# The shared expert of all batches worked in the last turn and behind the experts, with new turn orders; last results fetched by SyncE

## The chip, the cores and the metric

The kernel runs on one core of a Trainium2 chip. A core has TensorE (PE: matrix products, from SBUF into the eight banks of PSUM), VectorE (DVE), ScalarE (ACT), GpSimd (POOL) and SyncE (SP). Each works its instructions in the order in which they are written, and waits on counters (semaphores) that others raise. Data between HBM and SBUF go by DMA, issued by SP, ACT or POOL. The metric is the device time of one execution in microseconds (us).

## What is computed

Eight batches of 256 tokens with 256 channels go through four steps, each followed by a layer norm of input plus result:

```
x = layernorm(x + L0_attn(x))   # q, k, v; convolution of 3; long convolution by FFT; Wo
x = layernorm(x + L0_ffn(x))    # 16-head causal attention, modulated MLP of 1024
x = layernorm(x + L1_attn(x))   # q * cumsum(k * v), Wo
x = layernorm(x + L1_ffn(x))    # mixture of experts, below

probs = softmax(x @ gate_w.T);  topk_w, topk_idx = top_k(probs, 6)      # of 64 experts
routed_out = sum over the 6 of topk_w * (silu(x @ w1[e].T) @ w2[e].T)   # inner width 176
g, u = split(x @ shared_gate_up.T)                                      # 352 each
shared_out = silu(g) * u @ shared_down.T                                # the shared expert
return routed_out + shared_out
```

Everything is in float32 but for a few split operands.

## The kernel before

**Turns.** The first three steps and the routing are a pipeline over batches. Stage A is the first step, C and B the second (C: the queries and keys; B: units u0 to u15 of attention, MLP f0 to f7, B8), D the third step with routing, G the scatter of the rows of a routed batch to their experts' places in HBM. One turn works A of batch n, B of n-1, D of n-2 and G of n-3. A table of part names (`TURN`) sets the order, and each engine runs those of its parts that stand in it. There are turns -1 to 9. Turn 1 has its own table (no D yet), turn 8 is `LAST_BUT_ONE` (no A), turn 9 is `LAST` (only D and G). So D, and with it the shared expert, stands in turns 2 to 9.

**Attention units.** In a unit TensorE makes scores (L772), DVE their maxima (L1340), ACT the exponentials (L1070), DVE the reciprocal of their sums, POOL multiplies (`prob<-prob,rec`, L564). Three units later TensorE transposes (L659) and ACT copies (probT), and one unit further TensorE makes the values (L790, L796). The G scatters (L589) stand between POOL's multiplies, as do the inverse roots of the norms (L572: yA, yB, yD, yR).

**The shared expert.** x3, the output of step three, is transposed to x3T. S0, S1 and S2 are gate and up products in tiles of 128, 128 and 96 columns (L893, bank 7), each with a tanh on ACT (L1124) and two products on DVE (L1458, L1461) that give sact. SDa and SDb are the down product (L912), SD adds it to x3 into X (L1490). In the last turn S0 stands between DTa and DTb, the two parts that work out the table of experts for the chunks; the others stand behind DTb.

**Behind the turns.** SP waits for the table to load expert weights, and for the last scatter (D6, 12 scatters of batch 7 from x_row) to load rows. 40 quads of 4 chunks of 128 rows follow: transposes (L659), inner products (L962, L968), outer products (L979, L983), the scatter of the results to y_rows by POOL (L627). At last 16 tiles are finished: ACT issues the load of a tile's six results per token (`collect`, L1149), makes diagonal weights (`weigh`, L1157) and issues the store (`put`, L1166), all in one queue; TensorE sums five of the six (L995), DVE adds the sixth, X and the sum (L1589, L1592) and norms. There are four load buffers and two output buffers (`outb`).

Of the kernel before, what the change touches and what calls it, by code (L numbers as in the profile page):

```python
# [28 lines left out]
P = 128  # L29
NB, L, D = 8, 256, 256  # L30
KT = D // P
# [101 lines left out]
def build(nc, d):  # L133
# [6 lines left out]
    with ExitStack() as ctx:  # L140
# [96 lines left out]
        sgt, sgs, sact = sb("sgt", [P, L]), sb("sgs", [P, L]), sb("sact", [P, len(SH_TILES), L])  # L237
        hit = sact[:].rearrange("p n l -> p (n l)").rearrange("p (t k e) -> p t k e", t=TT, k=TOPK)

        zeros = sgt  # L240
# [17 lines left out]
        def ring(n, *shape):  # L258
# [25 lines left out]
            "d_rank d_pos d_dest d_copied d_scat d_sg d_sgt d_sact d_sd d_base "  # L284
            "ch_a ch_b ch_d ch_r ch_f r_tot r_tab r_row r_table r_fill "
            "m_w0 m_x0 m_w1 m_x1 m_w2 m_x2 m_w3 m_x3 m_ids ch_m r_spot r_all m_xT m_xT_out m_h m_hs m_y m_y_out m_st0 m_st1 m_st2 m_st3 "
            "f_ld0 f_ld1 f_ld2 f_ld3 f_st0 f_st1   f_diag f_sum f_r f_out n_varF n_invF").split()}
# [17 lines left out]
        class Chain:  # L305
# [20 lines left out]
        TURN = """u0 A3a u1 G0 D1 A3b u2 G1 D2k A3p u3 G2 D2x u4 G3 D2v D2q u5 G4 D2w A4a u6 G5 D3 u7 G6 D3n A4b A4z u8 G7 D3o A5 u9 G8 D4 A5n  # L326
            u10 G9 A5o S0 u11 G10 D4l A6n S1 u12 G11 D4m A6o S2 u13 D4t u14 SDa SDb SD u15 B6a B6c B6b C1 f0 D4k f1 C2 f2 D5 f3 D5p C2v
            f4 D4w D5h f5 f6 Z1 f7 Z1b C2h Zq Zk B8 D6 Z2""".split()
# [4 lines left out]
        LAST_BUT_ONE = """u0 u1 G0 D1 u2 G1 D2k u3 G2 D2x u4 G3 D2v D2q u5 G4 D2w u6 G5 D3 u7 G6 D3n u8 G7 D3o u9 G8 D4 u10 G9 S0 u11 G10 D4l S1  # L333
            u12 G11 D4m S2 u13 D4t SDa u14 SDb SD u15 B6a B6c B6b f0 D4k f1 f2 D5 f3 D5p f4 D4w D5h f5 f6 f7 B8 D6""".split()


        LAST = "D1 G0 G1 G2 G3 G4 G5 D2k D2x D2v D2q D2w D3 D3n G6 G7 G8 G9 G10 G11 D3o D4 D4l D4m D4t D4k D5 D5p D5h D6 DTa S0 DTb S1 S2 D4w SDa SDb SD".split()
        LAG = {"Z": -1, "A": 0, "C": 0, "B": 1, "D": 2, "G": 3}
        STAGE = {"u": "B", "f": "B", "S": "D"}

        def turns(eng, parts):
# [16 lines left out]
            turn(NB + 1, LAST)  # L358

# [47 lines left out]
        def tile_loop(eng, skewed):  # L407
# [11 lines left out]
            for off in range(NT, NT + len(skewed) - 1):  # L419
                step(0, off)  # L420

# [19 lines left out]
        def _(sp):  # L441
# [93 lines left out]
            quad_loop(sp, [load], begin=2)  # L535

# [104 lines left out]
        def _(pe):  # L641
# [242 lines left out]
            def shared(n):  # L884
                at, w = SH_TILES[n]
                def part(b):
                    if n:
                        need(pe, "d_sact", b * 3 + n)
                    else:
                        pe.wait_ge(S["d_x3T_out"], b + 1)  # L890
                    for g in range(2):
                        for kt in range(KT):
                            mm = pe.matmul(bank[0:w, 7, g * L:(g + 1) * L], sh_gu[:, kt, g * SH_I + at:g * SH_I + at + w],  # L893
                                           x3T[:, kt, :], start=(kt == 0), stop=(kt == KT - 1))
                    mm.then_inc(S["d_sg"], 1)
# [10 lines left out]

            def shared_out(tt):
                def part(b):
                    if tt == 0:
                        pe.wait_ge(S["d_sact"], b * 3 + 3)  # L910
                    for n, (_, w) in enumerate(SH_TILES):
                        mm = pe.matmul(psum(7, tt * D, (tt + 1) * D), sact[0:w, n, tt * P:(tt + 1) * P], sh_dn[0:w, n, :],  # L912
                                       start=(n == 0), stop=(n == len(SH_TILES) - 1))
                    if tt == TT - 1:
                        mm.then_inc(S["d_sd"], 1)
                return part
# [18 lines left out]

# [722 lines left out]
```

## Time and profile before

| | us |
|---|---|
| runs | 1130.39, 1128.96, 1128.15 |
| median | 1128.96 |
| profiled execution | 1125.7 |
| its span, first to last instruction | 1123.9 |
| mean granted clock of TensorE | 0.944 |
| PE busy | 962.8 (86%) |
| DVE busy | 650.4 (58%) |
| POOL busy | 461.6 (41%) |
| ACT busy | 341.8 (30%) |

The busy times are of one profiled execution. Turns last to about 785 us, experts from 789 to 1059, the last 16 tiles from 1073 to the end. Numbers such as L893 are lines of the kernel before.

### The profile page before, as it was taken

Reading aid. Unit: us, or ns where it says so; the run is one execution under the profiler, and the core shown is the slowest. Engines: PE = TensorE matmul, PEld = TensorE weight load, DVE = VectorE, ACT = ScalarE, POOL = GpSimd, SP = SyncE. Lnnn points to the kernel's source line nnn. Section 1 sums busy time; section 2 is a strip of 40 time slices with the busy share of each in tenths; the row PEclk is TensorE's granted clock in tenths of the full one; section 3 lists DMA queues with packets and bytes.
Section 4 is the critical chain, followed back from the end, with each engine's and each line's share of the span. In section 5 each row is a group of like instructions: output and inputs, shape, how many; then the busy total and the mean of one; then the engine's idle time right before and its main releaser. Section 6 shows DMA issues by size and latency. Waiting matters only on the chain. (4 is left out here: it accounts for less than half of the span.)

```text
span 1123.9 us, 20566 instructions
## 1 busy us (share of the span) xinstructions
PE 962.8 (86%) x6315; PEld 787.1 (70%) x6315; DVE 650.4 (58%) x2103; ACT 341.8 (30%) x1034; POOL 461.6 (41%) x508
## 2 busy tenths in 40 slices
PE   4466889998998999999999988844999999999676
PEld 3354677786786787787777766733788888888554
DVE  2833535776776776677677645644455555555356
ACT  1023424425425426326335335100111111111333
POOL 0412313217417317218228236054265666566612
PEclk8878889999999999999999989977899999999989
DMA  9229990050050051051041141015987888879286
GB/s 358 99 64 306 274 220 2 1 123 35 26 122 34 24 121 39 19 121 43 14 113 49 47 91 44 1 58 195 348 296 265 287 265 271 278 230 315 87 302 224
DMA packets 102899, 163.26 MB, mean 145 GB/s; under 512 B 26848, under 2 KB 76992, under 8 KB 100416
## 3 DMA queue, kind: packets, MB, share of 16 engines
q1 hardware_dynamic: 83312, 111.34, 34.6%
q0 software_dynamic: 12288, 33.96, 8.0%
q10 hardware_dynamic: 7248, 17.32, 4.3%
q8 instruction: 26, 0.43, 0.2%
q14 instruction: 25, 0.20, 0.1%
HBM read 139.32 MB, written 61.87 MB: 179 GB/s over the span
## 5 line engine op out<-in xcount | busy, mean ns | idle before, releaser
L564 POOL TENSOR_TENSOR prob<-prob,rec 128x512 f32<-128x512 f32 x96 | 100.9, 1052 | 84.8 <-DVE rec L1346 83.9
L1070 ACT ACTIVATE prob<-bank,nmx 128x128 f32<-128x128 f32 (+1 forms) x256 | 104.7, 427 | 63.7 <-DVE nmx L1340 62.9
L1340 DVE TENSOR_REDUCE nmx<-bank 128x2 f32<-128x512 f32 (+1 forms) x96 | 65.4, 687 | 70.4 <-PE bank L772 63.0
L589 POOL DMA_INDIRECT x_rows<-x_copy,desti x84 | 87.0, 1035 | 15.7 <-issue 15.7
L1063 ACT ACTIVATE probT<-bank 128x512 f32<-128x512 f32 x96 | 57.3, 597 | 72.2 <-PE bank L659 71.1
L579 POOL TENSOR_TENSOR products<-z,products 128x512 bf16<-128x512 f32 x8 | 9.2, 1152 | 147.2 <-ACT products L1051 147.2
L831 PE MATMUL bank<-h2T,w_up 128*128 128x256 f32 x256 | 67.9, 388 | 0.0
L833 PE MATMUL bank<-h2T,w_in 128*128 128x256 f32 x256 | 66.1, 381 | 0.0
L659 PE MATMUL bank<-cst,prob 128*128 128x128 f32 x384 | 59.5, 279 | 5.0 <-ACT probT L1063 4.8
L893 PE MATMUL bank<-x3T,sh_gu 128*128 128x256 f32 (+1 forms) x192 | 51.5, 415 | 10.1 <-DVE sact L1461 8.1
L844 PE MATMUL bank<-w_down,actT 128*128 128x256 f32 x256 | 56.6, 379 | 0.0
L1070 ACT ACTIVATION_READ_ACCUMULATOR prob<-bank,nmx 128x1 f32 x256 | 54.6, 213 | 0.0
L833 PEld LDWEIGHTS bank<-h2T,w_in 128*128 128x128 f32 x256 | 49.1, 192 | 6.9
L844 PEld LDWEIGHTS bank<-w_down,actT 128*128 128x128 f32 x256 | 48.5, 190 | 6.8
L659 PEld LDWEIGHTS bank<-cst,prob 128*128 128x128 f32 x384 | 45.2, 144 | 11.4 <-issue 5.8
L1092 ACT ACTIVATE gt<-bank 128x256 f32<-128x256 f32 x64 | 24.5, 383 | 92.4 <-PE bank L836 87.3
L1367 DVE SCALAR_TENSOR_TENSOR gs<-gt,bank 128x256 f32<-128x256 f32 x64 | 26.8, 418 | 43.7 <-ACT gt L1092 43.7
L831 PEld LDWEIGHTS bank<-h2T,w_up 128*128 128x128 f32 x256 | 46.5, 195 | 7.4
L572 POOL TENSOR_TENSOR yB<-vB,minus_half 128x2 f32<-128x2 f32 x8 | 5.7, 710 | 109.3 <-DVE vB L1196 109.3
L893 PEld LDWEIGHTS bank<-x3T,sh_gu 128*128 128x128 f32 (+1 forms) x192 | 35.7, 196 | 19.8 <-DVE sact L1461 10.1
L1136 ACT ACTIVATE kc<-bank 128x384 f32<-128x384 f32 x20 | 9.8, 490 | 125.8 <-PE bank L968 125.8
L1575 DVE COPY d_kv<-bank 128x512 f32<-128x512 f32 x20 | 13.8, 691 | 59.1 <-PE bank L983 59.1
(385 smaller groups left out, 2458.4 us busy)
## 6 DMA issues: line engine op xcount, KB each, us to landing
w_in<-in_e_w SPq DMA_DIRECT2D x20, 448.0 KB
w_up<-in_e_w SPq DMA_DIRECT2D x20, 448.0 KB
w_down<-in_e_w SPq DMA_DIRECT2D x20, 448.0 KB
products<-in_e_w SPq DMA_DIRECT2D x20, 448.0 KB
prob<-in_e_w SPq DMA_DIRECT2D x20, 448.0 KB
probT<-in_e_w SPq DMA_DIRECT2D x20, 448.0 KB
actT<-in_e_w SPq DMA_DIRECT2D x20, 448.0 KB
x_rows<-sgt SPq DMA_DIRECT2D x1, 8320.0 KB, 38.4
```

What stands on the lines that cost most here:

```text
L564: pool.tensor_tensor(p, p, r, ALU.mult).then_inc(S["b_scaled"], 1)
L589: pool.indirect_dma_start(x_rows, bass.IndirectOffsetOnAxis(ap=desti[:, n:n + 1].bitcast(U32), axis=0), rows[:, n // TOPK, :], None).then_ ...
L659: return pe.transpose(out, x, ident)
L831: pe.matmul(psum(n, L, 2 * L), w_up[:, kt, cols], h2T[:, kt, :], start=(kt == 0), stop=(kt == KT - 1))
L833: pe.matmul(psum(n, 0, L), w_in[:, kt, cols], h2T[:, kt, :], start=(kt == 0), stop=False)
L844: mm = pe.matmul(psum(1, tt * D, (tt + 1) * D), actT[:, f, tt * P:(tt + 1) * P], w_down[:, f, :], start=(f == 0), stop=(f == FT - 1))
L893: mm = pe.matmul(bank[0:w, 7, g * L:(g + 1) * L], sh_gu[:, kt, g * SH_I + at:g * SH_I + at + w], x3T[:, kt, :], start=(kt == 0), stop=(kt ...
L1063: act.activation(probT[:, turned % PROBTS, :, :], bank[:, 2, :].rearrange("p (j q) -> p j q", j=4), ACT.Copy).then_inc(S["b_pT_out"], 1)
L1070: i = act.activation(prob[:, u % PROBS, h * w:(h + 1) * w], psum(u % 2, h * w, (h + 1) * w), ACT.Exp, bias=nmx[:, u, h:h + 1], accum_out=s ...
L1092: act.activation(gt[:, f % 2, :], psum((0, 2, 3)[f % 3], 0, L), ACT.Tanh, scale=0.5).then_inc(S["b_gt"], 1)
L1340: dve.tensor_reduce(nmx[:, u, 0:512 // w], bank[:, u % 2, :].rearrange("p (h k) -> p h k", k=w), AX, ALU.max, negate=True).then_inc(S["b_m ...
L1367: cbn.link(dve.scalar_tensor_tensor(gs[:, f % 2, :], gt[:, f % 2, :], 1.0, psum(n, 0, L), ALU.add, ALU.mult))
```

## The change

The shared expert leaves the turns. In its place ACT copies x3 into X (part D4). In the last turn, parts `L<n>x` transpose batch n's rows of X again into one of two buffers lx, `L<n>0` to `L<n>2` are gate and up products (now in banks 2 and 3 in turn) with tanh and the two DVE products, and `L<n>o` is the down product (banks 4 and 5) with the add into X. Batches 0 to 5 stand in `LAST` among the parts of D of batch 7; batches 6 and 7 run behind the last expert (`BEHIND_EXPERTS`). The buffers are those of stages A and C, which are free then. `hit` and `zeros` get space of their own. `TURN` has another order too. The loads of the last 16 tiles are issued by SP, and there are four output buffers in use.

```diff
-        LAST = "D1 G0 G1 G2 G3 G4 G5 D2k D2x D2v D2q D2w D3 D3n ... D6 DTa S0 DTb S1 S2 D4w SDa SDb SD".split()
+        LAST = """G0 G1 L0x G2 G3 L00 G4 D1 L01 G5 D2k D2x D2v D2q L1x D2w L02 D3 L0o D3n G6 ...
+            ... D5 D5p D5h D6 L2o L31 DTa DTb L32 L4x L40 L3o L41 L42 L5x L50 L4o L51 L52 D4w L5o""".split()
+        BEHIND_EXPERTS = "L6x L60 L61 L7x L62 L70 L6o L71 L72 L7o".split()
@@ SyncE
+            def collect(c):
+                s = c.slot(YG)
+                need(sp, "f_r", c.no - (YG - 1))
...
+                sp.dma_start(yg[s], y_rows[rows, :].rearrange("(p k) d -> p k d", k=TOPK)).then_inc(S[f"f_ld{s}"], 16)
+            sp.wait_ge(S["m_y"], 2 * QUADS)
+            for s in range(4):
+                sp.wait_ge(S[f"m_st{s}"], 32 * (QUADS // 2))
+            tile_loop(sp, [collect])
@@ TensorE
+            def late_rows(n):
+                def part(b):
+                    if n < NB - 1:
+                        pe.wait_ge(S["d_base"], n + 1)
+                    need(pe, "l_xT_out", n)
+                    if n == 0:
+                        pe.wait_ge(S["b_r"], NB)
+                    turn_tiles(psum(1), slots(X, n)).then_inc(S["l_xT"], 1)
+                return part
+
+            def late_gate(n, k):
+                at, w = SH_TILES[k]
+                def part(b):
+                    if k == 0:
+                        pe.wait_ge(S["l_xT_out"], n + 1)
+                    need(pe, "l_sact", n * 3 + k - 1)
                     for g in range(2):
                         for kt in range(KT):
+                            mm = pe.matmul(bank[0:w, 2 + (n * 3 + k) % 2, g * L:(g + 1) * L], sh_gu[:, kt, g * SH_I + at:g * SH_I + at + w],
+                                           lx[n % 2][:, kt, :], start=(kt == 0), stop=(kt == KT - 1))
+                    mm.then_inc(S["l_sg"], 1)
+                return part
+
+            def late_out(n):
+                def part(b):
+                    pe.wait_ge(S["l_sact"], n * 3 + 3)
+                    need(pe, "l_add", n - 1)
...
+            pe.wait_ge(S["m_y_out"], 2 * QUADS)
+            behind_experts(late)
             tile_loop(pe, [add_up])
@@ ScalarE
             def D4(b):
...
                 act.activation(x3T[:], psum3(7), ACT.Copy).then_inc(S["d_x3T_out"], 1)
+                act.activation(slots(X, b), x3, ACT.Copy).then_inc(S["d_base"], 1)
...
-            tile_loop(act, [collect, None, None, None, put])
+            behind_experts(late)
+            tile_loop(act, [weigh_next, None, None, put])
@@ VectorE
+            def late_gate(n, k):
...
+                    cl.link(dve.scalar_tensor_tensor(lsgs[...], lsgt[...], 1.0, bank[0:w, to, 0:L], ALU.add, ALU.mult))
...
+            def late_out(n):
+                def part(b):
+                    dve.wait_ge(S["l_sd"], n + 1)
+                    dve.tensor_tensor(slots(X, n), psum3(4 + n % 2), slots(X, n), ALU.add).then_inc(S["l_add"], 1)
+                return part
```

On POOL, in a steady turn before, from the seventh multiply of the probabilities (`prob<-prob,rec`) on, with the scatters and the roots yD, yA and yR:

```order
L564 TENSOR_TENSOR prob<-prob,rec 128x512
L589 DMA x_rows<-x_copy,desti 147584x264
L572 TENSOR_TENSOR yD<-vD,minus_half 128x2
L564 TENSOR_TENSOR prob<-prob,rec 128x512
...
L572 TENSOR_TENSOR yR<-vR,minus_half 128x2
L564 TENSOR_TENSOR prob<-prob,rec 128x512
L589 DMA x_rows<-x_copy,desti 147584x264
```

The same stretch now:

```order
L589 TENSOR_TENSOR prob<-prob,rec 128x512
L597 TENSOR_TENSOR yD<-vD,minus_half 128x2
L589 TENSOR_TENSOR prob<-prob,rec 128x512
L614 DMA x_rows<-x_copy,desti 147584x264
...
L589 TENSOR_TENSOR prob<-prob,rec 128x512
L597 TENSOR_TENSOR yR<-vR,minus_half 128x2
L614 DMA x_rows<-x_copy,desti 147584x264
```

The root yD now stands ahead of the seventh multiply and its scatter, and yR behind the last multiply instead of ahead of it.

On TensorE, at the start of the last turn before (x and x_row are stage D's, their transposes L659, L880 the logits):

```order
L844 MATMUL bank<-w_down,actT 128x256 x16
L659 MATMUL bank<-cst,x 128x128 x4
L646 MATMUL bank<-x2T,d_wk 128x256 x4
L646 MATMUL bank<-x2T,d_wv 128x256 x4
L646 MATMUL bank<-x2T,d_wq 128x256 x4
L654 MATMUL bank<-d_wo,d_k 128x256 x4
L659 MATMUL bank<-cst,x_row 128x128 x4
L880 MATMUL bank<-gate_w,x3T 128x64 x4
```

The same stretch now; `cst,X` are the transposes of a deferred batch, `sh_gu` its gate and up products, `sh_dn` its down product:

```order
L927 MATMUL bank<-kv,sh_gu 96x256 x4
L679 MATMUL bank<-d_wo,d_k 128x256 x4
L938 MATMUL bank<-sh_dn,q_sb 128x256 x2
...
L927 MATMUL bank<-kvT,sh_gu 128x256 x8
L684 MATMUL bank<-cst,X 128x128 x4
L684 MATMUL bank<-cst,x_row 128x128 x4
L927 MATMUL bank<-kvT,sh_gu 96x256 x4
L927 MATMUL bank<-kv,sh_gu 128x256 x4
...
L905 MATMUL bank<-gate_w,x3T 128x64 x4
```

Between the output product of D and its logits there stand now two down products, five gate products and a transpose.

On TensorE at the table, before (L922 the totals of DTa, L928 and L933 the table row and the experts of DTb):

```order
L922 MATMUL bank<-seen,csb 128x64
L893 MATMUL bank<-x3T,sh_gu 128x256 x4
L928 MATMUL bank<-cst,ctab 1x128 x4
L933 MATMUL bank<-mk,csb 128x128 x2
L893 MATMUL bank<-x3T,sh_gu 128x256 x4
```

And now:

```order
L927 MATMUL bank<-kvT,sh_gu 128x256 x4
L956 MATMUL bank<-seen,csb 128x64
L962 MATMUL bank<-cst,ctab 1x128 x4
L967 MATMUL bank<-mk,csb 128x128 x2
L927 MATMUL bank<-kvT,sh_gu 96x256 x4
```

Nothing stands between the totals and the table row any more.

## Rows read from the trace of the kernel before

**Rows 1.** The page's 40 slices of 28 us, in tenths: TensorE, its clock, DMA.
```profile
PE   4466889998998999999999988844999999999676
PEclk8878889999999999999999989977899999999989
DMA  9229990050050051051041141015987888879286
```

**Rows 2.** Windows of a steady turn and the last but one: stretch, length, busy us.
```profile
core 0: us, PE busy (x) PEld busy (x) DVE busy (x) ACT busy (x) POOL busy (x), PEclk, DMA share, GB/s
381.71:463.49 81.78, 76.03 (x488) 62.05 (x484) 56.73 (x164) 34.73 (x109) 35.01 (x35) 1.00 0.24 62
626.54:703.74 77.20, 67.49 (x420) 52.82 (x416) 42.14 (x129) 31.34 (x102) 30.78 (x31) 0.91 0.23 63
```

**Rows 3.** The same turn, of L893 alone and then of L912 alone.
```profile
381.71:463.49 81.78, 5.91 (x24) 4.10 (x24) 1.00 0.24 62
381.71:463.49 81.78, 2.76 (x12) 2.20 (x12) 1.00 0.24 62
```

**Rows 4.** Timeline of POOL in that turn: start, us, engine, line, operation [idle before].
```profile
423.66 1.04 POOL L564 TENSOR_TENSOR prob<-prob,rec 128x512 f32<-128x512 f32 x1 [2.98 <-DVE rec L1346]
...
442.58 0.72 POOL L572 TENSOR_TENSOR yD<-vD,minus_half 128x2 f32<-128x2 f32 x1
...
456.60 1.04 POOL L564 TENSOR_TENSOR prob<-prob,rec 128x512 f32<-128x512 f32 x1 [0.19 <-DVE rec L1346]
```

**Rows 5.** Timeline of TensorE in that turn.
```profile
417.90 1.99 PE L703 MATMUL bank<-kvT,fwd 128*128 128x256 f32 x8 [0.39 <-ACT kvT L1030]
...
421.29 0.65 PE L659 MATMUL bank<-cst,x 128*128 128x128 f32 x4 [0.95 <-DVE x L1201]
...
456.50 1.97 PE L893 MATMUL bank<-x3T,sh_gu 128*96 128x256 f32 x8 [0.95 <-DVE sact L1461]
...
460.22 2.76 PE L912 MATMUL bank<-sh_dn,sact 128*128 128x256 f32 x12
462.91 0.65 PE L796 MATMUL bank<-probT,v 128*32 128x128 f32 x16
...
467.77 0.28 PE L836 MATMUL bank<-m_stack,b_stack 128*128 128x256 bf16 x1 [0.56 <-DVE m_stack L1358]
```

**Rows 6.** Timeline of TensorE in the last turn, to the first expert transpose.
```profile
733.87 1.12 PE L659 MATMUL bank<-cst,x 128*128 128x128 f32 x4 [4.45 <-DVE x L1201]
735.67 3.38 PE L646 MATMUL bank<-x2T,d_wk 128*128 128x256 f32 x8 [0.69 <-ACT x2T L1098]
...
763.87 3.76 PE L893 MATMUL bank<-x3T,sh_gu 128*128 128x256 f32 x8
...
770.93 2.80 PE L893 MATMUL bank<-x3T,sh_gu 128*128 128x256 f32 x8
775.18 1.97 PE L893 MATMUL bank<-x3T,sh_gu 128*96 128x256 f32 x8 [1.45 <-DVE sact L1461]
778.52 2.86 PE L912 MATMUL bank<-sh_dn,sact 128*128 128x256 f32 x12 [1.37 <-DVE sact L1461]
789.03 1.12 PE L659 MATMUL bank<-cst,fwd 128*128 128x128 f32 x4 [7.64 <-DMA v<-x_rows]
```

**Rows 7.** Window from the MLP's end to the first expert transpose.
```profile
729.40:789.02 59.62, 26.89 (x101) 19.45 (x100) 26.88 (x114) 4.74 (x9) 26.25 (x29) 0.72 0.36 129
```

**Rows 8.** VectorE in the last turn: the places of the last scatter; a shared-expert product (group).
```profile
763.53 0.17 DVE L1485 CAST desti<-destf 128x12 int32<-128x12 f32 x1
...
L1461 DVE SCALAR_TENSOR_TENSOR sact<-sgs,bank 128x256 f32<-128x256 f32 x2 | 0.8, 421 | 0.1
```

**Rows 9.** Timeline of the last 16 tiles: TensorE, VectorE, ScalarE's DMA queue, VectorE.
```profile
1072.77 4.21 PE L995 MATMUL bank<-w_in,stack_q 128*128 128x256 f32 x10 [13.85 <-DMA w_in<-y_rows]
1077.09 0.42 DVE L1592 TENSOR_TENSOR qc<-qc,bank 128x256 f32<-128x256 f32 x1 [3.86 <-PE bank L995]
...
1081.66 0.35 ACTq L1149 DMA_DIRECT2D w_up<-y_rows  x1
...
1116.94 0.42 DVE L1592 TENSOR_TENSOR qc<-qc,bank 128x256 f32<-128x256 f32 x1
```

More of the change, by code:

```diff
@@ L358, in turns, with behind_experts @@
             turn(NB + 1, LAST)
+        def behind_experts(parts):
+            for name in BEHIND_EXPERTS:
+                if name in parts:
+                    parts[name](NB - 1)
         class Quad:
@@ L420, in tile_loop, with slots @@
                 step(0, off)
+        def slots(t, b):
+            return t[:, b * TT:(b + 1) * TT] if isinstance(b, int) else t[:, bass.ds(b * TT, TT)]
         def tile_of(t, n):
@@ L1115, in D4m, with late_rows @@
                 i.then_inc(S["d_ex"], 1)
[L1117 to L1118 removed]
+            def late_rows(n):
                 def part(b):
[L1120 to L1125 removed]
+                    act.wait_ge(S["l_xT"], n + 1)
+                    need(act, "l_sg", (n - 1) * 3)
+                    act.activation(lx[n % 2][:], psum3(1), ACT.Copy).then_inc(S["l_xT_out"], 1)
+                return part
+            def late_gate(n, k):
+                at, w = SH_TILES[k]
+                def part(b):
+                    act.wait_ge(S["l_sg"], n * 3 + k + 1)
+                    need(act, "l_sact", n * 3 + k - 1)
+                    act.activation(lsgt[(n * 3 + k) % 2][0:w, :], bank[0:w, 2 + (n * 3 + k) % 2, 0:L], ACT.Tanh, scale=0.5
+                                   ).then_inc(S["l_sgt"], 1)
+                return part
+            late = {**{f"L{n}x": late_rows(n) for n in range(NB)}, **{f"L{n}{k}": late_gate(n, k) for n in range(NB) for k in range(3)}}
             turns(act, {"Z1": biased(("q", q_sb, 2, 4, "a_qc")), "Z1b": biased(("k", k_sb, 2, 5, "a_kc"), ("v", v_sb, 0, 4, "a_kv")),
@@ L1129, in _ @@
                         **{f"u{u}": unit(u) for u in range(UNITS + BEHIND)}, **{f"f{f}": mlp(f) for f in range(FT)},
-                        **{f"S{n}": shared(n) for n in range(3)}})
+                        **late})
             def silu(c):
@@ L1485, in D5h @@
                 dve.tensor_copy(desti[:].rearrange("p (t k) -> p t k", t=TT), destf[:]).then_inc(S["d_dest"], 1)
-            def SD(b):
-                dve.wait_ge(S["d_sd"], b + 1)
-                for tt in range(TT):
-                    i = dve.tensor_tensor(slot(b, tt), psum(7, tt * D, (tt + 1) * D), x3[:, tt, :], ALU.add)
-                i.then_inc(S["d_base"], 1)
             cr = Chain(dve, "ch_r", 0)
@@ L1534, in DTb @@
                 cr.link(dve.tensor_copy(expert_of.rearrange("p (c k) -> p k c", k=2), psum3(6)[:, :, 0:P]))
+            late = {**{f"L{n}o": late_out(n) for n in range(NB)}, **{f"L{n}{k}": late_gate(n, k) for n in range(NB) for k in range(3)}}
             turns(dve, {"DTa": DTa, "DTb": DTb, "Zq": conv("q", q_sb, qc), "Zk": conv("k", k_sb, kc), "A3p": A3, "A4z": A4, "A5n": A5, "A5o": A5o,
@@ L1539, in _ @@
                         "D2v": D2, "D2w": D2w, "D3n": D3, "D3o": D3o, "D4m": D4m, "D4t": D4t, "D4k": D4k, "D4w": D4w, "D5p": D5p, "D5h": D5h,
-                        **{f"S{n}": shared(n) for n in range(3)}, "SD": SD})
+                        **late})
             for ch in (ca, cbn, cd):
```

121 lines of the change are left out of this document (50 added, 71 removed).

## The prediction

> **What bounds the kernel now.** I read the 40 slices first: TensorE is at 8 or 9 tenths through the turns (200 to 700 us) and the experts (from 790), and falls to 4 at two places, the last turn (740 to 790) and the step behind the experts (1060 to 1075), where its clock falls too [rows 1]. The windows by turn say how full "full" is: a steady turn takes 81.8 us with TensorE busy for 76.0; the last but one takes 77.2 at a mean clock of 0.91 [rows 2]. The windows of the two shared-expert lines give what is to be moved: 5.91 us for the gate and up products (L893) and 2.76 us for the down product (L912) in each turn [rows 3], and its third product stood 0.95 us for the shared expert's own product on VectorE (456.50, [rows 5]). The experts are TensorE's alone and untouched: I leave them out of the sum.
>
> **The turns: seven carry a shared expert (the D stage of batches 0 to 6).** The most that one can give back is 5.91 + 2.76 + 0.95 = 9.6 us. What is late next is POOL. It multiplies the probabilities of the 12 units, with the 12 scatters of an older batch between them: the first multiply starts at 423.66, the last ends at 457.64 [rows 4], 34.0 us in which 12 multiplies at 1.04, 11 scatters at about 1.2 with their gaps, the two table products (2.5) and three roots (0.72 each) leave it 3.6 idle. The new order takes the root yR out from before the last multiply, but puts the root yD in front of the seventh multiply instead of behind it, and the table products in front of a scatter that filled a gap. Walking POOL's queue with these durations and the time at which yD's input was there (442.58, [rows 4]), I get the last multiply's end at 455.6: 2.0 us earlier. Behind it stand the last transposes, the probT copy and the last values (462.91, [rows 5]): 5.3 us from POOL's end, since TensorE is inside the shared expert meanwhile. Without it: transposes 0.15 + 0.6, copy 0.65, so 1.45 us; 3.8 earlier. Together 5.8 us a turn. The rest of the turn hangs on b_mh (467.77, [rows 5]), 3.3 us behind the gather product; VectorE now scales xn just ahead of it, which the same 3.3 us hold. Bounds: 2.0 (POOL alone, the tail not shortened) and 9.6. Six turns at 5.8 make 34.8. The last but one keeps its old order but for the shared parts; its first gate product was slow, it waited for rows that the others hide, but it already runs partly at half clock and will be emptier: I take 6. Sum: **-41 us** (-14 to -67). ScalarE's added copy of x3 into X (0.6 us) and the copy of the transposes lie beside an engine that is 42% busy in a turn (34.7 of 81.8 us, [rows 2]).
>
> **The last turn.** Before, from the end of the MLP (729.40) to the first expert transpose (789.03, [rows 6]) it took 59.6 us, TensorE busy for 26.9 at a mean clock of 0.72 [rows 7]. Of these the shared expert of batch 7 made 3.76 + 2.80 + 1.97 + 2.86 = 11.4 [rows 6], so D stage and table 15.5, or 15.5 x 0.72 = 11.2 at full clock. Now six batches are worked here. One costs 5.91 + 2.76 + 0.6 for four transposes = 9.3, less some 0.15 by which each of six groups begins before the modelled end of the one ahead (460.22 + 2.76 is 462.98, and the values begin at 462.91, [rows 5]): 8.4; six make 50.4. To 61.6 come waits that the order leaves: 1.4 until x is there (733.87), 2.0 at the transposes of x3, 0.9 at the ranks, 1.3 at the totals, 6.2 between totals and table row (nothing of L stands between DTa and DTb on TensorE, where before a gate product stood), 1.7 at the last down product: 13.5. Behind the 6.2 the clock will be down: the gate products that ran behind such waits took 3.76 and 2.80 instead of 1.97 [rows 6], so 2.7 more. Sum 77.8, against 59.6: **+18 us**, ending at 807.
>
> Beside it runs the path by which it ended before: POOL's 12 scatters of the last batch begin at desti (763.53, [rows 8]) and lead over their landing and the row loads to the first transpose at 789.03, 25.5 later. The D chain is now stretched, as every step on TensorE and VectorE has parts of L ahead of it: the batch-0 down product and its add before the moments (+3.1), two VectorE parts before x3 (+1.4), three TensorE groups before the logits (+4), two VectorE parts between the ranks and the positions and one in the mask (+2.9, at 0.42 for each of two instructions, [rows 8]); less what full clock gives (-0.7). So desti is 10.7 late and rows are there at 800, under the cover of TensorE's 807. If L took nothing of TensorE, the turn would still cost 10.7; if it takes half clock through its first half, 25 products at +0.2 to 0.4 us, 28. Bounds +11 to +28.
>
> Here a rule of the Trainium skill speaks against the change ("TensorE: Matmul & The Clock Gate", section "HAM oscillation"): idle gaps of TensorE drop its clock to half for what follows. The trace agrees at this place: the first projection took 3.38 one group behind a wait of 4.45 [rows 6]. By it the last turn should get cheaper, being full, and the turns dearer, being emptier; the second is a rival below.
>
> **Behind the experts.** TensorE's last expert product ends at 1058.9; the fetched results arrive at 1072.77 [rows 9]. In these 13.9 us two batches (16.8 us of TensorE) now run, with 0.8 until VectorE has copied the last result and 2.6 of waits in the chain of the last down product: the first summing starts at 1079.1. Before, it ran at half clock, 4.21 us, and the first tile was complete at 1077.51; now it takes 2.3 and VectorE adds at 1081.9: 4.4 later. From there the tiles ran one in 2.66 us (1077.51 to 1117.36, 15 of them, [rows 9]). ScalarE did three things in one queue, so the sixth tile's load went out at 1081.66, 4.2 us behind the first tile's sum, where its buffer was free after 2.2. SyncE issues it at once, and four output buffers take the wait for the store away. TensorE needs 2.2 a tile, but the DMA engines were already at 8 to 9 tenths [rows 1], so I take 2.37 a tile: -4.4. **0 us**, bounds -3 (2.2 a tile) and +4.4 (2.66 kept). The Trainium skill ("Trainium Kernel Development and Optimization", section "Key Constraints") says that issuing from several engines only saves the sequencer's issue time, since all share the DMA engines. By that rule the stage costs the whole +4.4; the rows show a load held back by other work in its queue, not by issue time.
>
> **Sum.** -41 + 18 + 0 = -23 on a profiled execution of 1125.7 us (span 1123.9). The runs shown have a median of 1128.96, 3.3 above; the same difference on that gives 1106.
>
> **Rivals.**
> A. TensorE alone bounds the turns and POOL gives way: 8.6 us in each of seven, -60, and the last turn full-clocked at +15: -45, 1084. For: 3.6 idle on POOL, TensorE had 76 of 82. Against: the walk of POOL's queue. Chance 0.20.
> B. The clock falls in the turns. The transposes of x stand ahead of the first transform now, so the transform's 1.8 us no longer fill the time before x: the waits of 0.39 and 0.95 become one of about 3.1 [rows 5]. If the next groups go at half clock, as a projection did with 1.4 more [rows 6], 2 us are lost a turn: +14, 1120. Chance 0.14.
> C. Slower: POOL takes the turns over entirely. Its last multiply comes only 2.0 earlier and the tail is filled with waits for A6o and the softmax, so seven turns give 14; the last turn costs 18 and the tail 2: +6, 1135. It decides when a turn gives less than 2.9 us. Chance 0.09.
> D. The fetching by SyncE brings nothing: 1106 + 4.4 = 1110. Chance 0.07.
> The forecast has 0.50, with its own range 1095 to 1116 (a turn at 4.5 to 7, the last turn at +15 to +22).
>
> The range for all, 1084 to 1120, leaves out half of A, C and the rim of B. Below 0.2% (2 us) nothing can be told from no change. Faster: the forecast, A, D and nearly all of B, 0.90; same 0.02; slower 0.08.
>
> **What would show it.** In the profile after: turns of 76 us (72 in A, 78 in B with a clock under 1.0, 80 in C); POOL's last multiply 2 us earlier against the MLP's end; between the last MLP's end and the first expert transpose 78 us with a gap of 6 us ahead of the table row, TensorE's last down product ending it and not a row load; the expert stage as long as before; 20 us from the last expert product to the first summing, and tiles 2.4 apart. I am wrong if the turns are shortened by less than 4 or more than 7.5 us, or if the last turn ends on the row loads.

## Result and the profile after

| | before | after |
|---|---|---|
| runs, us | 1127.09 to 1130.39 | 1140.12 to 1143.72 |
| median, us (4 runs each) | 1128.56 | 1142.07 |
| profiled execution, its span | 1125.7, 1123.9 | 1140.12, 1138.3 |
| mean granted clock | 0.944 | 0.932 |
| PE busy, us | 962.8 | 983.7 |

The ratio after to before is 1.0118, 95% interval 1.0096 to 1.0141: slower by 1.2%, where a faster kernel of 1106 us was forecast; the time lies outside the range of 1084 to 1120 too. TensorE is busy for 21 us more although it has the same products to make and only four transposes a batch more: it works them at a lower mean clock.

The 40 slices of the page after (28.5 us each, tenths: TensorE, its clock, DMA), to be laid beside [rows 1]:

```profile
PE   5466899889789889888988987997999999999996
PEclk8777899999889899889899889998999999999999
DMA  9229990051041051141131221006887878879276
```

The two holes of before, at the last turn and behind the experts, are filled: between the first four digits and the last none is under 7. But the turns, which stood at 9 with the clock at 9, are now mostly at 8 with a clock of 8 or 9.

Windows after (columns as in [rows 2]; the slowest of the five steady turns, the last but one, the last from the MLP's end to the first expert transpose):

```profile
462.96:547.04 84.08, 74.18 (x452) 59.34 (x448) 55.35 (x155) 34.22 (x107) 34.99 (x35) 0.91 0.22 60
629.68:699.75 70.07, 59.50 (x384) 45.80 (x380) 39.29 (x119) 30.43 (x100) 30.90 (x31) 0.91 0.26 68
725.14:802.67 77.53, 63.45 (x304) 51.61 (x305) 41.61 (x147) 14.59 (x31) 26.24 (x29) 0.96 0.37 125
```

This steady turn has 36 products fewer and is 2.3 us longer than the one in [rows 2], 81.78; the mean of the five grew by 1.7, from 81.7 to 83.3. The last but one lost the same parts, kept its order, and got 7.1 shorter, from 77.20. The last grew by 17.9, from 59.62 [rows 7].

Where the time went, by the two traces (a turn is read from one b_a product, which opens the MLP part, to the next; L816 before, L841 after):

| stretch | before | after | difference | forecast |
|---|---|---|---|---|
| to the second b_a product (turn 2) | 218.29 | 212.95 | -5.3 | -5.8 |
| five steady turns | 408.25 | 416.73 | **+8.5** | -29 |
| last but one | 77.20 | 70.07 | -7.1 | -6 |
| its MLP | 25.68 | 25.39 | -0.3 | 0 |
| last turn | 59.6 | 77.5 | +17.9 | +18 |
| experts | 269.9 | 268.6 | -1.3 | 0 |
| behind them | 65.0 | 67.0 | +2.0 | 0 |
| span | 1123.9 | 1138.3 | +14.4 | -23 |

One row holds the whole error: the steady turns, 37.5 us off. The first row is not to be read closer than about 3 us: e10 below, whose turns are those of before, reached the same product at 220.94 instead of 218.29.

TensorE at the head of that turn, after (compare [rows 5], the first two lines):

```profile
503.65 1.11 PE L684 MATMUL bank<-cst,x 128*128 128x128 f32 x4 [3.05 <-DVE x L1240]
504.55 3.62 PE L728 MATMUL bank<-kvT,fwd 128*128 128x256 f32 x8
...
508.82 2.34 PE L728 MATMUL bank<-kvT,fwd 128*128 128x256 f32 x8
511.00 1.89 PE L671 MATMUL bank<-x2T,d_wk 128*128 128x256 f32 x8
```

With the transposes of x ahead of the transform, TensorE waits 3.05 us with nothing to do, and the first half of the transform behind it runs at half clock: 3.62 us for what took 1.99. The projection of D begins 12.0 us behind the MLP's end, before 8.7.

TensorE at the tail, after:

```profile
540.65 1.08 PE L684 MATMUL bank<-cst,prob 128*128 128x128 f32 x4 [2.08 <-ACT probT L1101]
541.67 1.08 PE L821 MATMUL bank<-probT,v 128*32 128x128 f32 x16
544.25 1.09 PE L684 MATMUL bank<-cst,prob 128*128 128x128 f32 x4 [1.51 <-ACT probT L1101]
546.03 1.08 PE L821 MATMUL bank<-probT,v 128*32 128x128 f32 x16 [0.69 <-ACT probT L1101]
547.04 2.08 PE L841 MATMUL bank<-h2T,b_a 128*128 128x256 f32 x4
```

It waits for ScalarE's copies, and from 540.65 to 547.04 the granted clock is 0.50: the products of these lines take 1.08 us where they took 0.65 [rows 5]. What held the last two copies stands in ScalarE's queue, and behind it in VectorE's:

```profile
543.10 0.52 ACT L1153 ACTIVATE ex<-bank,nlg 128x64 f32<-128x64 f32 x2 [2.60 <-DVE nlg L1457]
543.51 0.60 ACT L1101 ACTIVATE probT<-bank 128x512 f32<-128x512 f32 x1
```

```profile
540.98 1.61 DVE L1347 TENSOR_SCALAR vR<-ms 128x2 f32<-128x2 f32 x1
542.51 0.22 DVE L1455 MAX8 lg<-bank 128x8 f32<-128x64 f32 x1
...
542.90 0.17 DVE L1457 TENSOR_SCALAR nlg<-lg 128x2 f32<-128x2 f32 x1
```

The gate's exponential (D4m) stands ahead of the second last probT copy, waits 2.60 us for the negated maxima nlg, and these stand on VectorE behind A6n, the part of stage A that makes the variance vR, of which POOL takes the root yR. Here vR took 1.61 us.

### The profile page after: what moved, and what is told of

Read it like the earlier page. It is cut to its first block, busy times and chain, and to the rows that moved or that the text cites. A ratio compares the mean times of both kernels' runs of the same rounds, so it can differ in the third digit from the quotient of the medians.

```text
span 1138.3 us, 20623 instructions
## 1 busy us (share of the span) xinstructions
PE 983.7 (86%) x6347; PEld 800.4 (70%) x6347; DVE 658.3 (58%) x2095; ACT 351.0 (31%) x1050; POOL 462.4 (41%) x508
## 4 chain that ended last, share of the span: by engine, by line
PE 60%; issue 15%; DVE 9%; SPq 6%; POOL 5%; ACT 3%; DMA 2%; ACTq 1%; DVEq 0%; POOLq 0%
PE bank L671 8%; PE bank L1019 7%; PE bank L998 6%; PE bank L684 6%; SPq L513 4%; PE bank L1015 4%; PE bank L1004 4%; PE bank L927 4%; PE bank L856 3%; PE bank L858 3%; PE bank L728 3%; PE bank L679 3%; PE bank L938 2%; PE bank L739 2%; POOL x_rows L614 1%
## 5 line engine op out<-in xcount | busy, mean ns | idle before, releaser
L589 POOL TENSOR_TENSOR prob<-prob,rec 128x512 f32<-128x512 f32 x96 | 100.7, 1050 | 77.1 <-DVE rec L1382 75.7
L684 PE MATMUL bank<-cst,prob 128*128 128x128 f32 x384 | 64.8, 295 | 38.6 <-ACT probT L1101 35.2
L856 PE MATMUL bank<-h2T,w_up 128*128 128x256 f32 x256 | 66.4, 382 | 0.0
L1130 ACT ACTIVATE gt<-bank 128x256 f32<-128x256 f32 x64 | 24.6, 384 | 90.1 <-PE bank L861 85.0
L305 POOL TENSOR_TENSOR spare<-ones_row 128x1 f32<-128x1 f32 x49 | 9.4, 191 | 100.6 <-DVE d_cs L1615 58.8
L1615 DVE COPY d_wq<-bank 128x512 f32<-128x512 f32 x20 | 13.8, 692 | 57.8 <-PE bank L1019 57.8
```

Source lines behind the costliest of these rows:

```text
L589: pool.tensor_tensor(p, p, r, ALU.mult).then_inc(S["b_scaled"], 1)
L684: return pe.transpose(out, x, ident)
L856: pe.matmul(psum(n, L, 2 * L), w_up[:, kt, cols], h2T[:, kt, :], start=(kt == 0), stop=(kt == KT - 1))
```

## The experiments

Fifteen kernels were run. I cut the turn at fixed points, since the total alone hides what moves against what. All from the traces, in us, of one steady turn each, the fourth of the five (463.49 to 545.26 in before): from the b_a product to the MLP's end; to POOL's first multiply of the probabilities; to the end of its last; to the next b_a product. Then comes the mean turn of the five (h1: of the four that kept their shared expert), and the last turn, where the text speaks of it. The kernels that are not in the table have the turns of e1 (e9, e8), of before (e10) or of e11 (b1); b2 stands in the text.

Each trace is of one execution. That of e6 was its slowest of ten (1132.0 us), that of e7 its fastest of ten (1121.6). The kernel before, measured beside each group again, had medians of 1126.0 to 1129.5, so kernels of different groups are better compared by their ratios than by their medians.

| kernel | median, ratio [95%] | MLP | to first | multiplies | tail | turn | mean turn | last turn |
|---|---|---|---|---|---|---|---|---|
| before | | 34.9 | 7.0 | 34.0 | 5.9 | 81.8 | 81.7 | 59.6 |
| after | 1142.1, 1.0118 | 36.0 | 7.0 | 36.5 | 4.5 | 84.1 | 83.3 | 77.5 |
| e1, old order | 1116.2, 0.990 [0.987, 0.993] | 36.4 | 7.0 | 33.0 | 2.0 | 78.3 | 78.4 | 78.0 |
| e2, new order, no deferral | 1140.3, 1.012 [1.008, 1.016] | 34.9 | 7.0 | 36.4 | 6.1 | 84.5 | 84.2 | |
| e3, old head | 1129.3, 1.002 [0.999, 1.004] | 36.3 | 7.0 | 33.1 | 4.5 | 80.9 | 81.0 | |
| e4, old tail | 1128.9, 1.001 [0.998, 1.004] | 35.9 | 7.0 | 36.2 | 2.9 | 82.0 | 81.0 | |
| e5, e1 and fillers | 1114.6, 0.988 [0.984, 0.991] | 34.9 | 7.0 | 33.0 | 3.1 | 77.9 | 77.8 | 78.0 |
| e6, e1 and D1 first | 1127.0, 0.997 [0.995, 1.000] | 36.3 | 7.0 | 36.3 | 2.3 | 81.8 | 81.0 | |
| e12, e6 and filled wait | 1116.1, 0.990 [0.987, 0.994] | 36.4 | 7.0 | 33.3 | 2.9 | 79.5 | 78.9 | |
| e7, e1 and A6n late | 1124.8, 0.997 [0.995, 0.999] | 36.5 | 7.0 | 32.3 | 4.5 | 80.3 | 79.8 | |
| e11, e7 and D4m late | 1110.4, 0.987 [0.982, 0.991] | 36.2 | 7.0 | 32.3 | 2.0 | 77.6 | 77.5 | |
| h1, four in turns | 1112.4, 0.988 [0.985, 0.992] | 34.9 | 7.1 | 34.1 | 5.9 | 82.0 | 82.4 | 63.6 |

**Order or deferral: e1 and e2.** e1 takes the changed kernel and gives `TURN` its old order, without the shared parts. e2 takes the kernel before and gives it the new order, with them.

```diff
-        TURN = """u0 u1 G0 D1 A3a u2 A3b A3p G1 D2k u3 ... D4l u12 A6n G11 D4m u13 D4t u14 u15 B6a B6c A6o B6b ...
+        TURN = """u0 A3a u1 G0 D1 A3b u2 G1 D2k A3p u3 ... D4l A6n u12 G11 D4m A6o u13 D4t u14 u15 B6a B6c B6b ...
```

> The changed kernel, but with the turn order of the kernel before (its parts of the shared expert taken out). Theory O (the new turn order lost what the deferral gave): the seven turns give back about 7 us each, as the last-but-one turn did (77.20 to 70.07), six more of them than now: six turns at 84.0 - 75 = 9 us, so -45 to -54 on 1142, 1090 to 1100. Rival T (the thin chain of multiplies, probT copies and values bounds a turn whatever the order): turns stay at 82 to 84 us and the time at 1135 to 1145.

> The kernel before, but with the new turn order; the parts of the shared expert stand at their old places in it. Theory O: the order alone costs, at the head a wait for x of 3 us and half clock behind it, at the tail waits for the probT copies, together 5 to 9 us in each of six turns less what the shared expert's products hide: +20 to +45, 1148 to 1175. Rival T: the order is neutral, 1126 to 1132.

e1: 1116.2, 26 below the changed kernel, but short of the 1090 to 1100. e2: 1140.3, +12, less than the +20 to +45. The new order costs with and without the deferral, and rival T is out. The deferral in the old order gives 12.5. A steady turn gives 3.2 there on the mean of five (408.25 to 392.17), not the 7 of the last but one, nor my 5.8.

**Which end: e3 and e4.** The same exchange, for the part of the turn up to u3 alone, then for the part behind it alone.

```diff
-        TURN = """u0 u1 G0 D1 A3a u2 A3b A3p G1 D2k u3 ...          (e3; the rest stays new)
+        TURN = """u0 A3a u1 G0 D1 A3b u2 G1 D2k A3p u3 ...
```

> The changed kernel with the old order in the first part of the turn only (up to unit 3). Theory O with the loss at the head: the wait of 3.05 us ahead of the transposes of x and the half clock of the transform behind it go, 3.3 us in each of six turns: -20, 1122. If the loss is at the tail alone: 1142, no change.

> The changed kernel with the old order in the second part of the turn only (from the scatter behind unit 3 on). Theory O with the loss at the tail (VectorE's queue holds the D4m and A6n parts, ScalarE's probT copies wait behind the gate's exponential, TensorE waits 5 us for probT and works the last values at half clock): 4 to 6 us in each of six turns: -25 to -35, 1107 to 1117. If the loss is at the head alone: 1142.

13 us each, 1129.3 and 1128.9: less than either had been expected to give (1122 and 1107 to 1117), but both ends cost, and the two halves make up the 26 of e1. The columns put each in its place: the old head takes the multiplies from 36.5 to 33.1, the old tail takes the tail from 4.5 to 2.9 or less.

**The head: e6 and e12.** D1 is the transposes of x; A3a and A3b are the halves of the transform. One move on e1, then the same with its wait filled by products that nothing reads (K, on TensorE, each 4 passes).

```diff
-        TURN = """u0 A3a u1 G0 D1 A3b u2 ...
+        TURN = """u0 u1 G0 D1 A3a A3b u2 ...           (e6)
+        TURN = """u0 u1 G0 K K K D1 A3a A3b u2 ...     (e12)
+            def K(b):
+                if first(b):
+                    return
+                for kt in range(KT):
+                    pe.matmul(psum(7, 0, L), sh_gu[:, kt, 0:P], x3T[:, kt, :], start=(kt == 0), stop=(kt == KT - 1))
```

> The kernel of the first run with one move at the head: the transposes of x (D1) stand ahead of the first transform (A3a), as in the new order; all else old. Theory H (the wait for x, 0.94 and 0.39 now, becomes one of 3 us, and half clock follows): +2.3 us in each of six turns, first to last multiply 35.2 instead of 33.0: 1128 to 1131. Rival (the cost of the new head is the later D2k, behind A3b and A3p): 1114 to 1118.

> The kernel with D1 ahead of A3a (first turn order otherwise old), and three pairs of filler products, 1.0 us each, on TensorE just ahead of D1, inside its wait of 3.05 us for x; their result is read by nothing. If the loss of that order (first to last multiply 36.2 us against 33.0) is the half clock behind the wait, the transform's two halves take 3.7 instead of 6.2 and the multiplies 33.7 to 34.2: turns 79.2 to 80, 1116 to 1120 against 1127. Rival (the wait itself moves the units' scores, whatever the clock): multiplies stay at 36, 1125 to 1129.

e6: 1127.0, the multiplies 36.3. e12: 1116.1, with the order of e6 and the multiplies 33.3. TensorE in e6:

```profile
499.79 1.11 PE L682 MATMUL bank<-cst,x 128*128 128x128 f32 x4 [3.05 <-DVE x L1238]
500.70 6.17 PE L726 MATMUL bank<-kvT,fwd 128*128 128x256 f32 x16
```

and in e12:

```profile
482.26 2.81 PE L945 MATMUL bank<-x3T,sh_gu 128*128 128x256 f32 x12
485.48 0.65 PE L682 MATMUL bank<-cst,x 128*128 128x128 f32 x4 [0.41 <-DVE x L1244]
485.97 3.62 PE L726 MATMUL bank<-kvT,fwd 128*128 128x256 f32 x16
```

x comes no sooner (4.64 us behind the MLP's end in both); 2.81 us of useless work in front of it make the 16 passes of the transform take 3.62 us instead of 6.17. The useless work is on no result's path, so nearly all the loss of this order is the clock and not the wait: 3.0 of the 3.3 us by which it lengthened the multiplies in this turn, 2.3 of 2.7 on the mean of the five. What stood behind the slow transform were the scores of the next units, for whose reciprocals POOL waits. POOL in e6, at its second multiply:

```profile
508.30 1.03 POOL L587 TENSOR_TENSOR prob<-prob,rec 128x512 f32<-128x512 f32 x1 [3.72 <-DVE rec L1380]
```

In e1 it did not wait there:

```profile
492.59 1.05 POOL L587 TENSOR_TENSOR prob<-prob,rec 128x512 f32<-128x512 f32 x1
```

The clock did not fall behind every such wait, though. In e4, which has the head of the changed kernel, the fifth steady turn went:

```profile
579.35 0.66 PE L682 MATMUL bank<-cst,x 128*128 128x128 f32 x4 [2.97 <-DVE x L1238]
579.84 1.89 PE L726 MATMUL bank<-kvT,fwd 128*128 128x256 f32 x8
...
582.01 1.95 PE L726 MATMUL bank<-kvT,fwd 128*128 128x256 f32 x8
```

The changed kernel, e2, e4 and e6 have 20 steady turns with this wait, each of 2.97 to 3.15 us. In three (this one, and two of e2) the 16 passes took 3.84 us, in the other 17 between 4.55 and 6.17. The multiplies of e4 took 32.9 us in this turn and 35.1 to 36.4 in its other four. So the same order costs little where the clock stays and over 3 us where it falls, which speaks for the clock once more; why it stayed in three turns, no run here shows.

**The tail: e7 and e11.**

```diff
-            ... G10 D4l A6n u12 G11 D4m A6o u13 D4t u14 u15 B6a ...
+            ... G10 D4l u12 A6n G11 D4m A6o u13 D4t u14 u15 B6a ...     (e7)
+            ... G10 D4l u12 A6n G11 A6o u13 u14 D4m u15 D4t B6a ...     (e11)
```

> The kernel of the first run with one move at the tail: A6n stands behind unit 12 instead of ahead of it; all else old. Theory V (VectorE's part of A6n then falls on a multiply of POOL and is held 1.4 us, the maxima of the logits come late, ScalarE's exponential of the gate waits 2.6 us instead of 0.9 with the last copies of probT behind it): +2 to +2.5 us in each of six turns, from the last multiply to the b_a product 4.5 instead of 2.0 to 2.9: 1126 to 1131. Rival (the cost of the new tail lies in A6o behind B6c, or in D3o, A5 and the scatters): 1114 to 1118.

> The kernel of the first run with A6n behind unit 12 (as in the kernel with A6n late), but D4m moved from unit 12 to behind unit 14 and D4t behind unit 15. Theory V (the tail's 4.5 us came from probT copies standing behind the gate's exponential in ScalarE's queue): they are released, from the last multiply to the b_a product 2.0 to 2.9 us again, first to last multiply stays 32.3, so turns of 77.5 to 78.5: 1111 to 1116. Rival (A6n itself, with its 1.4 us behind POOL's multiply, holds the tail): 4.5 stays, 1122 to 1128.

e7: 1124.8; the multiplies gain 0.6 and the tail goes to 4.5. e11: 1110.4; the multiplies keep their gain and the tail is 2.0 to 2.9 in the five steady turns. ScalarE in e7:

```profile
529.29 0.52 ACT L1151 ACTIVATE ex<-bank,nlg 128x64 f32<-128x64 f32 x2 [2.59 <-DVE nlg L1455]
529.70 0.60 ACT L1099 ACTIVATE probT<-bank 128x512 f32<-128x512 f32 x1
```

and in e11, where the exponential now comes behind the last copy:

```profile
520.07 0.60 ACT L1099 ACTIVATE probT<-bank 128x512 f32<-128x512 f32 x1 [1.31 <-PE bank L682]
521.48 0.52 ACT L1151 ACTIVATE ex<-bank,nlg 128x64 f32<-128x64 f32 x2 [0.81 <-DVE nlg L1455]
```

A6n is where it was in e7, and vR took as long:

```profile
517.75 1.61 DVE L1345 TENSOR_SCALAR vR<-ms 128x2 f32<-128x2 f32 x1
```

So A6n alone does no harm: it makes the maxima late, and they hurt through the exponential that stands ahead of the copies.

These two moves are not the whole of the new order. The mean steady turn of the changed kernel is 4.9 us longer than that of e1; the move at the head makes 2.5 of it (e6), the one at the tail 1.4 (e7). The other 1.0 (the places of D3, D3n, D3o, A5, A6o and some scatters, or the moves together) was not taken apart.

**The MLP's start: e5.** The same K behind units 13, 14 and 15 of e1.

```diff
-            ... u13 D4t u14 u15 B6a ...
+            ... u13 K D4t u14 K u15 K B6a ...
```

> The kernel of the first run (deferral, old turn order) with three pairs of products whose result nothing reads, some 0.9 us each at half clock and 0.5 at full, put on TensorE behind units 13, 14 and 15, where it waits for probT and prob. Theory C (TensorE's gaps at the turn's tail cost it the clock, and the MLP behind them pays: 36.3 us from the b_a product to the MLP's end against 34.9 before): the MLP part falls back to 34.9 to 35.3 and the turn from 78.4 to about 77.5: -3 to -7, 1109 to 1114. Rival F (the products cost what they take, and the clock of the MLP's start doesn't hang on them): MLP part stays 36.3, turns +0 to +1: 1116 to 1122.

A filler took 1.03 us, not the 0.5 that I had written. The MLP part is 34.8 to 34.9 in all five steady turns (e1: 36.2 to 36.4 in four of them) and the b_a product takes 1.03 us instead of 1.93 to 2.08; of these 1.4 us, 0.2 to 1.1 is lost in a tail of 3.05. Windows of the MLP in before, e1 and e5, in this order (length, TensorE's busy time; the clock is third from the end):

```profile
463.49:498.42 34.93, 34.37 (x173) 29.40 (x170) 24.63 (x74) 10.50 (x24) 3.30 (x3) 1.00 0.41 98
```

```profile
446.77:483.13 36.36, 36.03 (x173) 30.62 (x170) 24.16 (x72) 10.50 (x24) 3.31 (x3) 0.95 0.41 97
```

```profile
447.51:482.41 34.90, 34.27 (x170) 29.30 (x169) 24.15 (x72) 10.12 (x23) 3.30 (x3) 1.00 0.42 98
```

The same products in 34.4 and in 36.0 us: the shared expert, beside its work, had kept TensorE busy while POOL finished, and the MLP behind it ran at 2.4 GHz throughout. The medians, 1114.6 and 1116.2, are too near each other to tell the two kernels apart; the windows are what shows it.

**The last turn: e9, e8 and h1.**

```diff
-            ... DTa DTb L32 L4x L40 L3o L41 ...
+            ... DTa L32 L4x L3o L40 DTb L41 ...       (e9)
+            ... DTa L32 L4x L40 DTb L3o L41 ...       (e8)
```

> The kernel of the first run with one move in the last turn: L32, L4x, L3o and L40 stand between DTa and DTb instead of behind DTb. If the gap of 5.9 us between the totals and the table row costs the last turn what it lasts (TensorE is the bound there), 5 to 7 us go, with the half clock behind it: last turn 71 to 73 instead of 78.0, 1109 to 1111. Rival: the table comes later by what stands ahead of it, the path over the row loads takes over or the first expert waits for its weights, which SyncE loads behind the table: -2 to +3, 1114 to 1119.

> As the run with the filled gap, but between DTa and DTb stand only L32, L4x and L40, which wait for nothing behind VectorE's table work (L3o did: 4.88 us). Theory: their 4.5 us fill the gap of 5.9, about 1.2 stays and full clock with it: last turn 72 to 73.5 against 78.0 in the first run, 1110 to 1112. Rival (the gap moves to the next place that waits for VectorE behind its table work): last turn 76 to 78, 1113 to 1116.

TensorE between the two table parts, in the changed kernel:

```profile
769.39 0.19 PE L956 MATMUL bank<-seen,csb 128*128 128x64 bf16 x1 [1.18 <-DVE desti L1530]
775.45 1.87 PE L962 MATMUL bank<-cst,ctab 128*1 128x128 f32 x8 [5.87 <-DVE ctab L1564]
777.25 0.39 PE L967 MATMUL bank<-mk,csb 128*128 128x128 bf16 x2
777.43 2.83 PE L927 MATMUL bank<-kvT,sh_gu 128*96 128x256 f32 x8
```

In e9, then in e8:

```profile
751.02 1.22 PE L936 MATMUL bank<-sh_dn,k_sb 128*128 128x256 f32 x2 [4.88 <-DVE uT L1498]
```

```profile
747.31 1.03 PE L960 MATMUL bank<-cst,ctab 128*1 128x128 f32 x8 [0.96 <-DVE ctab L1562]
```

e9 put the down product L3o into the gap; it needs L32's product on VectorE, and VectorE works L32 behind the table. The gap only changed its name (4.88 us): last turn 77.1, only 0.9 less; the median is 1112.5 (0.986 [0.982, 0.989]), and what it has below e1 beyond that came in the last but one turn, 70.1 us instead of 73.1. e8 leaves only what waits for nothing on VectorE: last turn 71.1, 1107.0 (0.984 [0.980, 0.988]). The gap is paid in full: of the 6.9 us, 4.9 are the wait (5.87 to 0.96), and most of the rest is the half clock behind it (1.87 and 2.83 us for what takes 1.03 and 1.94).

h1 defers batches 0, 5 and 6 to the last turn and 7 behind the experts; 1 to 4, which are worked in a loop over turns, keep their shared expert where it was before.

```diff
+        LATE = (0, 5, 6, 7)
-        LAST = """G0 G1 L0x G2 G3 L00 G4 D1 L01 ...
+        LAST = "G0 G1 L0x G2 G3 L00 G4 D1 L01 G5 D2k D2x D2v D2q L02 D2w L1x D3 L0o D3n L10 G6 G7 G8 G9 G10 D3o L11 D4 SD G11 D4l
+            D4m D4t D4k L12 D5 D5p D5h D6 DTa L2x L1o L20 DTb L21 L22 D4w L2o"
+        BEHIND_EXPERTS = "L3x L30 L31 L32 L3o"
```

> Only the shared experts of batches 0, 5, 6 (in the last turn) and 7 (behind the experts) are deferred; those of batches 1 to 4 stay in their turns at the places of before, in the turn order of before. In the last turn L2x, L1o and L20 stand between DTa and DTb. Theory P (a shared expert costs a turn 3.3 us but the last turn and the step behind the experts 8.4): against the first run four turns lose 3.3 each (+13), the last turn falls from 78.0 to 58 to 61 (-18), one batch less stands behind the experts (-5): 1104 to 1109. Rival (the last turn is held by the rows' path, desti late, at 67 to 70): 1112 to 1118.

1112.4 lies in the rival's range, the last turn of 63.6 between the two (58 to 61, 67 to 70). Its window and the line that ends it:

```profile
712.99:776.55 63.56, 38.67 (x184) 30.72 (x184) 33.02 (x128) 8.82 (x18) 26.34 (x29) 0.88 0.34 121
```

```profile
776.56 1.11 PE L685 MATMUL bank<-cst,fwd 128*128 128x128 f32 x4 [9.89 <-DMA v<-x_rows]
```

Now the rows end it: desti at 750.67, 37.7 us behind the MLP's end (before 34.1), and 25.9 from there to the first transpose, as in [rows 6, 8]. A kept shared expert cost its turn 3.7 us in the turn of the table (82.0 against 78.3), 4.0 on the mean, and three fewer in the last turn gave 14.4, 4.8 each, since the path over desti takes over. One batch fewer behind the experts gave 5.6 us, where 5 were expected (60.8 from the last expert product to the end, e1 66.4), but the experts took 272.6 us in this trace, 4.0 more than in e1; what made them longer is open. By medians it stands 3.8 below e1 (1.9 by ratios) and 5.3 above e8.

**The last 16 tiles: e10.** The kernel before, with SyncE's loads and the four output buffers alone.

```diff
-            tile_loop(act, [collect, None, None, None, put])
+            tile_loop(act, [weigh_next, None, None, put])
+            tile_loop(sp, [collect])
```

> The kernel before with the change of the last 16 tiles alone: SyncE issues their loads, four output buffers. Theory of the prediction (a tile costs ScalarE's queue 2.66 us, then 2.37): -4.4, 1124. What the trace of the changed kernel showed (15 tiles in 37.8 us, 2.52 each): -2 to -3, 1126. Rival (DMA engines are the bound, the issuing engine is nothing): -0.5 to +0.5, 1128.5.

1126.2, ratio 0.9998 [0.9975, 1.0022]: no difference that can be measured. That is where the rival had put it, and the 4.4 us of the prediction are outside the interval. In its trace the 15 steps from the first to the last sum took 37.4 us, 2.49 each, where before took 39.85, 2.66 each. 2.5 us are within the interval, so the runs leave open whether they were there in every execution. Loads and buffers were changed together, so neither is shown to be the cause.

**The terms together: b1 and b2.** b1 has the order of e11 and the last turn of e8; b2 has K behind units 13, 14 and 15 too.

> All parts deferred as in the changed kernel, with the old turn order but for A6n behind unit 12, D4m behind unit 14 and D4t behind unit 15, and with L32, L4x and L40 between DTa and DTb. If the two gains add (0.9 us in each of six turns, 6.9 in the last turn): 1116 - 5 - 7 = 1104, 1100 to 1107. Rival (both came from the clock's history, not from the moves, and do not add): 1107 to 1111.

> The same with the three pairs of filler products behind units 13, 14 and 15 (their result is read by nothing). Theory C (full clock at the MLP's start, 1.4 us where the turn lacked it, less 0.2 to 1.0 that the fillers take of the tail): 2 to 4 below the other kernel of this call, 1098 to 1104. Rival F (with the shorter tail the fillers lie on the path): 0 to +3 above it.

b1: 1102.4, 0.977 [0.974, 0.981]. b2: 1103.1, 0.980 [0.977, 0.984]. b1 is faster than both kernels, by 24 and by 40 us, at the time that adding up had given. The fillers bring nothing on top: MLP 34.9, but tails of 3.1 to 4.7. With the tail short, useless work costs about what it restores: the mean steady turn is 77.6 in b2 and 77.7 in b1.

## Why the prediction was wrong

**The failed step: "Walking POOL's queue".** I walked the new POOL queue with the durations and input times of the old trace and got the last multiply 2.0 us earlier. In the very turn that I walked it came 1.3 later, measured from the first multiply (35.3 against 34.0), and on the mean of the five 1.8; in the turn of the table it was 2.5. The walk left the inputs where they were (only yD's was looked up), while the order moved the engines that make them. Two things broke it. At the head TensorE waits 3.05 us and in most turns is at half clock behind it, so the reciprocals come late: +3.3 (e6), of which the clock is 3.0 (e12). At the tail I counted "transposes 0.15 + 0.6, copy 0.65" (1.40, not the 1.45 written there) as if the copy had only its input to wait for; it stands in ScalarE's queue behind the gate's exponential (e7, e11). From POOL's end to the last values it was 3.5 us (542.56 to 546.03); in the old order of e1 it was 1.4, as counted.

**The term that I had at nothing: the MLP's start.** Taking 8.7 us of products out of the tail took the clock from the MLP, 1.4 us in four of five turns (e1 against e5). Even in the old order the turn of the table gives 3.5 (81.8 to 78.3, by -1.0 at the multiplies, -3.9 at the tail and +1.4), where 5.8 was forecast. In the trace of before this tail was full and its clock 1.00, but [rows 2] showed an emptier turn, the last but one, at 0.91.

**Rival B had the mechanism and the wrong size.** It named the one wait of about 3.1 us (3.05) and the half clock behind it, and priced it at 2 us a turn against a gain of 5.8. With up to 3.3 at the head, 2.5 at the tail and 1.4 at the MLP nothing was left of that gain. The only case on the slower side, C, had POOL's own queue as its cause, and POOL was late by what it waited for.

The Trainium skill's rule that I weighed ("TensorE: Matmul & The Clock Gate", section "HAM oscillation") says that idle gaps drop the clock for what follows. The traces agree in most turns: behind 3.05 us of wait half the transform took 3.62 for 1.99, and with the wait filled 16 passes took 3.62 for 6.17; but in three turns of 20 they took 3.84 behind the same wait. I had applied it to the last turn and made a rival of it for the turns; it belonged in the sum there.

**Right: the last turn.** +17.9 against +18, ended by the last down product at 802.67 and not by the rows; the gap ahead of the table row 5.87 against 6.2, with the products behind it at 2.83. The sum came out: 77.5 against 77.8, with TensorE idle for 14.1 of them (77.53 less 63.45), where the waits were put at 13.5. desti came at 769.08, 43.9 behind the MLP's end and so 9.8 later than before, where 10.7 was forecast.

**Nearly right: behind the experts.** The first summing came 19.9 us after the last expert product (20.2 forecast) and the first sum 4.1 later than before (4.4). Tiles came 2.52 apart instead of 2.37, so the stage cost 2.0 and not 0. The rule of the Trainium skill ("Trainium Kernel Development and Optimization", section "Key Constraints"), that several issuing engines save only issue time, would have had no gain at all per tile; the traces show 2.66 to 2.52 and 2.49, which the timing of whole runs (e10) neither confirms nor excludes. The 2.37 a tile of the prediction it does exclude.

**The sum as it should have stood.** The turns give 27 in the old order (e1's last MLP ends at 702.25, before at 729.40), the last turn takes 18 of them: 9 by the traces, 12.5 by the medians. The new order then cost 26, of which the steady turns hold 24.6 in the traces (5 times 4.9).

## What to carry to other kernels

Moving work off a busy engine frees only what its successors can use: read, for each queue that it leaves, what arrives late next, with the input times of the new order and not of the old. Count the clock as a term of its own, and with a range, wherever TensorE gets a hole (3.05 us here, which cost the multiplies of a turn 0.3 us in e4's fifth and 3.3 in e6's fourth, against e1), and place independent work in front of the wait. Read every steady turn of a trace before taking one for all. Into such a hole, put only what needs nothing of the engine that the hole waits for, and in an in-order queue put the side chain's instruction (here the gate's exponential) behind those of the main one.

## What the runs showed of the hardware

Useless products made a kernel faster: e12 against e6, 1116.1 to 1127.0 (ratios 0.990 and 0.997), by 2.81 us of work in a wait of each turn. A VectorE instruction on two columns took 1.61 us (vR at 540.98) where the same took 0.17 elsewhere (520.51 in e1). It ended at 542.59, and POOL's multiply at 542.56; in e7 the two ended at 528.78 and 528.75. POOL at that time:

```profile
541.50 1.06 POOL L589 TENSOR_TENSOR prob<-prob,rec 128x512 f32<-128x512 f32 x1
```

The Trainium skill ("SBUF — State Buffer", section "Who interferes with whom") says that VectorE's tensor_scalar can enter a mode in which it takes the port pair that it shares with GpSimd, and that whoever issues first holds the pair for its whole instruction while the other is blocked. The end times agree; that vR began 0.52 us ahead of the multiply and was held all the same is not explained by it. POOL was in a scatter when vR began (540.35 to 541.48), and the multiply followed on it; but the vR of e1 at 520.51 also ran inside a scatter (520.35 to 521.36) and took 0.17, so the scatter alone does not hold it. No run here took the multiply away.

Nor is the clock's cost the same from execution to execution, or from turn to turn. The last but one turn took 73.1 us in e1 and 70.4 in e8, whose orders up to there are equal; and behind the same wait at the head the five steady turns of e4 had multiplies of 32.9 to 36.4 us. In before, whose steady turns had a clock of 1.00, the five turns took 81.3 to 81.8.
